# Self-attention scores of a unit on two disjoint row groups of TensorE

## The chip, the cores and the metric

One core of one Trainium2 chip runs the kernel in a single launch. The metric is the device time of that core in microseconds (us). TensorE multiplies a stationary operand (loaded first, "PEld" in the profile) with a moving one (the matmul, "PE") into PSUM; VectorE (DVE), ScalarE (ACT) and GpSimd (POOL) work beside it, and SyncE (SP) issues the DMAs. Each engine takes its instructions in the order in which the kernel lists them and waits on semaphores.

## What is computed

Two layers of cross-attention run over x (4 batches, 1024 tokens, 512 features). The first layer attends to a context of 64 tokens. The second has a self-attention, an attention to the context and a gated feed-forward part. The change is in the self-attention, which the reference writes as (16 heads of 32 features, batch `b`, queries `i`, keys `j`):

```python
q = (x @ wq).reshape(b, n, H, DH).transpose(0, 2, 1, 3)      # DH = 32
k = (ctx @ wk).reshape(b, m, H, DH).transpose(0, 2, 1, 3)    # here ctx is x's own norm h1
sim = jnp.einsum('bhid,bhjd->bhij', _fq(q, dq, 128.0, 8), _fq(k, dk, 128.0, 8)) * SCALE
attn = jax.nn.softmax(sim, axis=-1)
out = jnp.einsum('bhij,bhjd->bhid', _fq(attn, dw, 0.0, 8), _fq(v, dv, 128.0, 8))
```

`_fq` rounds to 8-bit integers. The kernel keeps these integers of queries and keys as bf16.

## The kernel before

**Chunks.** The tokens are cut into 8 chunks of 512 (`CHUNKS`), two per batch, numbered n = 0 to 7. For each batch the program runs `cross(n)` for both of its chunks (first layer, norm, and the products q1, k1, v1), then for each of the two `self_attention(n)` and `middle(n)` (output product, second attention, norm). The feed-forward part of chunk n-1 is spread over `self_attention(n)` and `middle(n)`, by a plan written out by hand (`HOST`, `feed`); so chunk 0 has none beside it, and chunks 1 to 7 are called hosted here.

**Layout.** q1 and k1 stand as [128 rows, 4 groups, 1024 tokens]: a row is one feature, four heads of 32 rows make a group. Row 32h of group hg is where head 4*hg+h begins. So a score product has 32 rows of stationary queries (128 queries wide) and 32 rows of moving keys (512 keys).

**Self-attention.** A unit is one head and 128 queries against 1024 keys; a chunk has 64 units and 71 slots (`S_SLOTS`). In slot s the engines do, in order:
- TensorE (line 1711 on): two score products of unit s (line 1725), one per 512 keys, into two adjacent PSUM banks (0 and 1, or 2 and 3, by turns); eight transposes of unit s-5 (line 1734) into the one bank 4; in two slots of four, 16 small products with the values (line 1748); then the feed-forward quarters of the plan, each three products of 512 columns (lines 1461 to 1463). The score products wait until the exponential of unit s-2 has emptied their banks.
- VectorE (line 1335 on): the row maximum of unit s (line 1341), every second slot the scale and reciprocal of the sums (1347, 1349), and the copy of the transposed unit s-5 out of bank 4 (1360).
- ScalarE (line 1051 on): negated maximum (1056), exponential (1062), and feed-forward work.
- GpSimd (line 785 on): the product with the reciprocal (791).

**Rounding of q1, k1, v1** (`cross`, line 1322 on): ScalarE scales a finished product of 128x512 out of PSUM into one of two buffers `qt` (line 929), and VectorE takes it in two passes (`take_rounded`, 1188 and 1190) into q1, k1 or v1.

**The SP queue.** SyncE issues all loads in program order: weight blocks into three slots of SBUF (`load_block`, lines 536 to 550), feed-forward pieces (559, 560), and, for the first chunks, a preparation of weights: `load_prep` (613) loads, ScalarE (978) and GpSimd (743) split into a high and a low part, and `keep_prep` (626) stores. `cross(1)` ends with `keep_prep` of the eighth weight, and `self_attention(0)` begins with the block "o1" and the load of the ninth.

**An older pairing in the same kernel.** In the setup, `three_of_heads` (line 1513, the product at 1518) alternates between rows 0 to 63 and rows 64 to 127, each into a bank of its own.

Of the kernel before, what the change touches and what calls it, by code (L numbers as in the profile page):

```python
# [7 lines left out]
BF16 = mybir.dt.bfloat16  # L8
FP16 = mybir.dt.float16
ALU = mybir.AluOpType  # L10
# [3 lines left out]
P = 128  # L14
# [3 lines left out]
DK0, DH = 64, 32  # L18
CH = 512
NC = S // CH  # L20
# [3 lines left out]
HG = H // 4  # L24
FF = 2048
FT = FF // P
KEYT = S // P
UNITS = HG * NT * 4
CHUNKS = B * NC
STEPS0 = 2 * NT  # L30

ROUND = 12582912.0
# [15 lines left out]
PIECES = 2 * len(F_ORDER)  # L48
F_RING = 3
PIECE_END = [4 * (v // 2) + (3 if F_ORDER[v // 2][0] == "d" else 2 * (v % 2) + 1) for v in range(PIECES)]  # L50


LAG_T = 5
# [145 lines left out]
def build(nc, a, out):  # L199

    ctx = ExitStack()
    with ctx:
        def sb(name, shape, dt=F32):
            return ctx.enter_context(nc.sbuf_tensor(name, shape, dt))
# [4 lines left out]
        def signal(name, keys, by=1):  # L209
            return Signal(sem(name), keys, by)  # L210
# [84 lines left out]
        for i in range(F_RING):  # L295
# [11 lines left out]
        qt = [qt0, qt1]  # L307
        NE, NH = 5, 3
        bufs = scope([(f"e1_{i}", [P, S], F32) for i in range(NE)] + [(f"w1b_{i}", [P, S], FP16) for i in range(NH)]
                     + [(f"w1T_{i}", [P, KEYT, P], BF16) for i in range(8)])  # L310
        e1, w1b, w1T = bufs[:NE], bufs[NE:NE + NH], bufs[NE + NH:]
        bufs = scope([(f"e2_{i}", [P, H, SC], F32) for i in range(NT)] + [("q2T", [P, HG, CH], BF16)]
                     + [(f"w2b_{i}", [P, H * SC], FP16) for i in range(2)] + [(f"w2T_{i}", [P, PAIRS, P], BF16) for i in range(2)])
        e2, q2T, w2b, w2T = bufs[0:NT], bufs[NT], bufs[NT + 1:NT + 3], bufs[NT + 3:]
        sb("upper", [P, 44 * 256])

        w_hi, w_lo = [w0_hi, w1_hi, w2_hi], [w0_lo, w1_lo, w2_lo]
        psum = ctx.enter_context(nc.psum_tensor("psum", [P, 8, 512], F32))
# [27 lines left out]
        f_loaded = [sem(f"f_loaded{i}") for i in range(F_RING)]  # L346
        fbias_loaded = [sem(f"fbias_loaded{i}") for i in range(3)]
        batch_loaded = signal("batch_loaded", range(B), 7 * 16)
        p0_used = signal("p0_used", [(n, i) for n in chunks for i in range(NT)])
        w1T_used = signal("w1T_used", [(n, g) for n in chunks for g in range(UNITS // 4) if g % 4 < 3])  # L350
        xhi_done = signal("xhi_done", [(n, k) for n in chunks for k in range(KT)])
# [38 lines left out]
        def bank_of(key):  # L390
            return FILL[key][0]

        def bank(i):
            return psum[:, i, :]
# [6 lines left out]
        def wait_emptied(eng, key):  # L401

            i, n = FILL[key]
            eng.wait_ge(emptied[i], n + 1)
# [55 lines left out]
        def _(sp):  # L460
# [167 lines left out]
            def cross(n):  # L628

                b, c = divmod(n, NC)  # L630
                if c == 0:
                    load_batch(b)
                    load_x(n)
                for i in range(3):
                    load_fbias(n, i)
                if n == 0:
                    load_block((0, "M0"))
                    load_block((0, "N0"))
                    load_block((0, "M1"))
                if c == 0:  # L640
                    load_x(n + 1)
                if n < NC:
                    load_prep(PREP[4 * n])
                for i in range(3, 7):
                    load_fbias(n, i)
                load_block((n, "N1"))
                if n < NC:
                    keep_prep(PREP[4 * n])
                    load_prep(PREP[4 * n + 1])
                load_fbias(n, 7)  # L650
                load_block((n, "q1"))
                load_block((n, "k1"))
                if n < NC:
                    keep_prep(PREP[4 * n + 1])
                    load_prep(PREP[4 * n + 2])
                load_block((n, "v1"))
                if n < NC:
                    keep_prep(PREP[4 * n + 2])
                    load_prep(PREP[4 * n + 3])
                if c == 0:  # L660
                    load_block((n + 1, "M0"))
                    load_block((n + 1, "N0"))
                    load_block((n + 1, "M1"))
                elif n > NC:
                    wait_filled(sp, ("q1", n, 3))
                    for v in range(F_RING):
                        load_piece(n - 2, v)
                if n < NC:
                    keep_prep(PREP[4 * n + 3])

            def self_attention(n):

# [10 lines left out]
            def middle(n):  # L683

                last_of_batch = n % NC == NC - 1
                if n == 0:
                    for v in range(F_RING):
                        load_piece(0, v)
                for s in range(M_SLOTS):
                    if n >= 1:  # L690
                        feed(n - 1, HOST, S_SLOTS + s, not last_of_batch or n == CHUNKS - 1)
                    if s == 4:
                        load_block((n, "o2"))
                    if s == 10 and last_of_batch and n + 1 < CHUNKS:
                        load_block((n + 1, "M0"))
                    if s == 18 and n + 1 < CHUNKS:
                        if last_of_batch:
                            load_block((n + 1, "N0"))
                if n >= 1:
                    store_out(n - 1)  # L700
                if last_of_batch and n + 1 < CHUNKS:
                    load_block((n + 1, "M1"))
# [412 lines left out]
        def _(dve):  # L1115
# [104 lines left out]
            def quantise(key, dst):  # L1220

                r = rounds[0]
                rounds[0] += 1
                take_rounded(key, qt[r % 2][:], dst).then_inc(rounded.sem, 1)

            def residual(key, xt):

                wait_filled(dve, key)
                return emptied_bank(dve.tensor_tensor(xt, bank(bank_of(key)), xt, ALU.add), key)  # L1229
# [44 lines left out]
            def cross(n):  # L1274
# [47 lines left out]
                for m in range(HG):  # L1322
                    quantise(("q1", n, m), q1[:, m, here])
                for m in range(HG):
                    quantise(("k1", n, m), k1[:, m, here])
                for t in range(NT):
                    quantise(("v1", n, t), v1[:, n % NC * NT + t, :])

# [112 lines left out]
        def _(pe):  # L1441
# [9 lines left out]
            def wait_bank(i, key):  # L1451

                n = sum(1 for k in FILL if FILL[k][0] == i and ORDER[k] < ORDER[key])
                pe.wait_ge(emptied[i], n)
# [256 lines left out]
            def self_attention(n):  # L1711

                last = n // NC * NC + NC - 1
                pe.wait_ge(rounded.sem, rounded.at(("v1", last, 3)))
                wait_bank(1, ("s1", n, 0))
                wait_bank(3, ("s1", n, 0))
                for s in range(S_SLOTS):
                    if s < UNITS:

                        hg, t, h = s // 16, s // 4 % 4, s % 4  # L1720
                        p = slice(DH * h, DH * h + DH)
                        q = n % NC * CH + t * P
                        wait_empty(("s1", n, s))
                        for i in range(2):
                            ins = pe.matmul(bank(bank_of(("s1", n, s)) + i), q1[p, hg, q:q + P], k1[p, hg, 512 * i:512 * i + 512],  # L1725
                                            start=True, stop=True)
                        done(ins, ("s1", n, s))
                    u = s - LAG_T
                    if 0 <= u < UNITS:
                        key = ("p1T", n, u)  # L1730
                        pe.wait_ge(w1_ready.sem, w1_ready.at((n, u)))
                        wait_empty(key)
                        for k in range(KEYT):
                            ins = pe.transpose(bank(bank_of(key)).bitcast(FP16)[:, k * P:k * P + P],  # L1734
                                               w1b[u % NH][:, k * P:k * P + P], ident16[:])
                        done(ins, key)
                    g, part = divmod(s - LAG_T - 4, 4)
                    if 0 <= g < UNITS // 4 and part < 2:
                        hg, t = divmod(g, 4)
                        key = ("a1", n, hg)  # L1740
                        if part == 0:
                            wait_emptied(pe, ("p1T", n, 4 * g + 3))
                            if t == 0:
                                wait_empty(key)
                        for k in range(4 * part, 4 * part + 4):
                            for h in range(4):
                                hd = DH * (4 * hg + h)
                                ins = pe.matmul(bank(5)[DH * h:DH * h + DH, t * P:t * P + P], v1[:, k, hd:hd + DH],  # L1748
                                                w1T[4 * (g % 2) + h][:, k, :], start=(k == 0), stop=(k == KEYT - 1))
                        if part == 1:  # L1750
                            if t == 3:
                                done(ins, key)
                            else:
                                ins.then_inc(w1T_used.sem, 1)
                    if n >= 1:
                        feed(n - 1, HOST, s)
# [108 lines left out]
```

## Time and profile before

| | |
|---|---|
| median of 3 runs | 3900.94 us (3900.22 to 3907.26) |
| the profiled execution, its own time | 3903.09 us |
| its span, first to last instruction | 3901.3 us |
| mean granted clock of TensorE | 0.872 of 2.4 GHz |

The profile counts as busy only compute instructions, and the end of a matmul is modelled, so that successive matmuls overlap in it. "Granted clock" 1.00 is 2.4 GHz and 0.50 is 1.2 GHz. "x2" merges two instructions of the same kind that follow each other. "<-" names what ended an engine's idle time. The chain of waits follows the work back from the last instruction.

### The profile page before, as it was taken

What the parts mean: (1) busy time and instruction counts of PE and PEld (TensorE: products, weight loads), DVE (VectorE), ACT (ScalarE), POOL (GpSimd) and SP (SyncE); (2) the same over time, 40 slices, a digit from 0 to 9 for tenths busy, and PEclk for the clock granted to TensorE, in tenths of its full rate; (3) what the DMA queues carried; (4) which work ended last, traced back from release to release, by engine and by line L of the source; (5) the groups of instructions that cost most, each with busy time, mean ns of one, the idle gap of its engine ahead of it and who ended that gap; (6) DMA issues with size and microseconds to landing.
All of it is one profiled execution on the core that took longest, in us unless ns stands there. A gap on an engine that the chain in (4) does not pass through costs nothing.

```text
span 3901.3 us, 50803 instructions
## 1 busy us (share of the span) xinstructions
PE 3174.2 (81%) x19712; PEld 2210.8 (57%) x19712; DVE 2174.1 (56%) x3559; ACT 1624.8 (42%) x2666; POOL 1328.8 (34%) x1025
## 2 busy tenths in 40 slices
PE   4445658789968799989967799889977799989989
PEld 4334433445656555655756655655756555655767
DVE  2324538667455567467445557467455567467431
ACT  3312136447422267357422257346422267357421
POOL 1231326344331234244241234244231244244231
PEclk8677765669988889999988879989988899999999
DMA  6873543312343322322344322322343322322334
GB/s 211 287 279 154 191 172 130 130 54 77 130 150 138 133 105 77 140 103 82 150 136 150 132 76 76 141 98 77 131 151 142 133 98 76 141 108 77 133 127 173
DMA packets 227694, 514.00 MB, mean 132 GB/s; under 512 B 96512, under 2 KB 113152, under 8 KB 205440
## 3 DMA queue, kind: packets, MB, share of 16 engines
q1 hardware_dynamic: 215040, 509.14, 35.8%
q10 hardware_dynamic: 12416, 1.62, 0.3%
q8 instruction: 158, 2.59, 0.3%
q14 instruction: 80, 0.66, 0.1%
HBM read 428.39 MB, written 82.31 MB: 131 GB/s over the span
## 4 chain that ended last, share of the span: by engine, by line
PE 62%; DVE 13%; issue 7%; POOL 6%; ACT 5%; DMA 4%; SPq 2%; ACTq 1%; POOLq 0%; DVEq 0%
PE psum L1461 17%; PE psum L1462 15%; PE psum L1463 15%; PE psum L1734 6%; PE psum L1725 6%; DVE mx L1341 2%; PE psum L1748 2%; DVE stats L1233 1%; POOL w1b L791 1%; DMA kept<-st_lo 1%; DVE w1T L1360 1%; POOL rstd L749 1%; DVE x L1229 1%; DVE den L1347 1%; ACT e L1062 1%
## 5 line engine op out<-in xcount | busy, mean ns | idle before, releaser
L791 POOL TENSOR_SCALAR w1b<-e,rec 128x1024 f16<-128x1024 f32 x512 | 572.8, 1119 | 903.9 <-DVE rec L1349 751.0
L1341 DVE TENSOR_REDUCE mx<-psum 128x1 f32<-128x1024 f32 x512 | 625.5, 1222 | 326.6 <-PE psum L1725 323.0
L1062 ACT ACTIVATE e<-psum,nb,scale 128x1024 f32<-128x1024 f32 x512 | 616.6, 1204 | 16.7
L1461 PE MATMUL psum<-h_hi,fw_hi 128*128 128x512 f32 x1024 | 463.7, 453 | 2.1 <-DVE h_lo L1152 2.1
L1734 PEld LDWEIGHTS psum<-ident,w1b 128*128 128x128 f16 x4096 | 264.6, 106 | 329.7 <-issue 261.7
L1725 PE MATMUL psum<-k,q 32*128 32x512 bf16 x1024 | 355.6, 432 | 103.3 <-ACT e L1062 83.2
L1463 PE MATMUL psum<-h_hi,fw_lo 128*128 128x512 f32 x1024 | 422.1, 412 | 0.0
L1462 PE MATMUL psum<-h_lo,fw_hi 128*128 128x512 f32 x1024 | 421.3, 411 | 0.0
L1734 PE MATMUL psum<-ident,w1b 128*128 128x128 f16 x4096 | 356.7, 237 | 72.1 <-DVE w1T L1360 60.7
L1360 DVE TENSOR_SCALAR w1T<-psum 128x1024 bf16<-128x1024 f16 x512 | 347.1, 678 | 44.2 <-PE psum L1734 42.8
L1461 PE MATMUL psum<-w_hi,ht_hi 128*128 128x512 f32 x640 | 268.8, 420 | 74.2 <-DVE e L1287 39.4
L1056 ACT ACTIVATE nb<-mx,nscale 128x1 f32<-128x1 f32 x512 | 150.0, 293 | 410.1 <-DVE mx L1341 409.2
L1229 DVE TENSOR_TENSOR x<-psum,x 128x512 f32<-128x512 f32 x224 | 152.6, 684 | 272.2 <-PE psum L1463 272.2
L1462 PE MATMUL psum<-w_lo,ht_hi 128*128 128x512 f32 x640 | 260.7, 407 | 0.0
L1463 PE MATMUL psum<-w_hi,ht_lo 128*128 128x512 f32 x640 | 259.1, 405 | 0.0
L1461 PE MATMUL psum<-fw_hi,u_hi 128*128 128x512 f32 x512 | 229.9, 449 | 21.4 <-POOL u_lo L800 15.9
L749 POOL TENSOR_TENSOR rstd<-ve,mhalf 128x1 f32<-128x1 f32 x128 | 87.0, 679 | 467.7 <-DVE ve L1237 467.7
L1461 PEld LDWEIGHTS psum<-h_hi,fw_hi 128*128 128x128 f32 x1024 | 203.1, 198 | 74.3 <-issue 27.0
L1152 DVE TENSOR_TENSOR ht_lo<-psum,ht_hi 128x512 fp32r<-128x512 f32 x160 | 108.2, 689 | 222.5 <-ACT psum L985 121.8
L1463 PEld LDWEIGHTS psum<-h_hi,fw_lo 128*128 128x128 f32 x1024 | 204.3, 200 | 48.1
L1725 PEld LDWEIGHTS psum<-k,q 32*128 32x128 bf16 x1024 | 57.5, 95 | 297.1 <-issue 183.9
L1462 PEld LDWEIGHTS psum<-h_lo,fw_hi 128*128 128x128 f32 x1024 | 205.7, 201 | 27.9
(165 smaller groups left out, 5763.5 us busy)
## 6 DMA issues: line engine op xcount, KB each, us to landing
fw_hi<-pieces SPq DMA_DIRECT2D x192, 512.0 KB, 3.2
fw_lo<-pieces SPq DMA_DIRECT2D x192, 512.0 KB, 4.2
w_hi<-kept SPq DMA_DIRECT2D x80, 1024.0 KB, 4.9
w_lo<-kept SPq DMA_DIRECT2D x80, 1024.0 KB, 7.4
fbias<-in_fside_Bx16xSxS SPq DMA_DIRECT2D x64, 256.0 KB, 4.1
prep_raw<-in_L_xattn_ff_w SPq DMA_DIRECT2D x12, 1024.0 KB, 8.1
pieces<-prep_hi SPq DMA_DIRECT2D x24, 512.0 KB, 3.6
pieces<-prep_lo SPq DMA_DIRECT2D x24, 512.0 KB, 5.6
```

The lines of the kernel that those rows point to most:

```text
L749: pool.tensor_tensor(rstd[:, t:t + 1], ve[:, t:t + 1], mhalf[:, t:t + 1], ALU.pow).then_inc(rstd_ready.sem, 1)
L791: pool.tensor_scalar(w1b[u % NH][:], e1[u % NE][:], rec1[:, u % 8:u % 8 + 1], HALF, ALU.mult, ALU.add).then_inc(w1_ready.sem, 1)
L1056: act.activation(nb1[:, s % 4:s % 4 + 1], mx1[:, s % 4:s % 4 + 1], ACT.Copy, scale=nscale[:, 0:1]).then_inc(nb_ready.sem, 1)
L1062: act.activation(e1[s % NE][:], psum[:, i:i + 2, :].rearrange("p i n -> p (i n)"), ACT.Exp, bias=nb1[:, s % 4:s % 4 + 1], scale=scale[:, 0:1],
L1229: return emptied_bank(dve.tensor_tensor(xt, bank(bank_of(key)), xt, ALU.add), key)
L1341: dve.tensor_reduce(mx1[:, s % 4:s % 4 + 1], psum[:, i:i + 2, :].rearrange("p i n -> p (i n)"), AX, ALU.max).then_inc(maxed1.sem, 1)
L1360: emptied_bank(dve.tensor_scalar(w1T[u % 8][:].rearrange("p k q -> p (k q)"), bank(bank_of(key)).bitcast(FP16), -HALF, W_HIGH, ALU.add, AL ...
L1461: pe.matmul(o, s_hi, m_hi, start=first, stop=False)
L1462: pe.matmul(o, s_hi, m_lo, start=False, stop=False)
L1463: return pe.matmul(o, s_lo, m_hi, start=False, stop=last)
L1725: ins = pe.matmul(bank(bank_of(("s1", n, s)) + i), q1[p, hg, q:q + P], k1[p, hg, 512 * i:512 * i + 512], start=True, stop=True)
L1734: ins = pe.transpose(bank(bank_of(key)).bitcast(FP16)[:, k * P:k * P + P], w1b[u % NH][:, k * P:k * P + P], ident16[:])
```

## The change

The second half of the keys (k1, columns 512 to 1023, the odd chunk of a batch) is stored 64 rows further on, modulo 128. A new buffer `q1_turned` holds a copy of the chunk's queries with their rows turned by 64 too. It shares SBUF with the end of weight slot 1. The two products of a unit then read rows 32h and 32(h^2): for h = 0 rows 0 to 31 and 64 to 95. The copy is made by two DMAs of SyncE per chunk (`turn_queries`); TensorE waits for them at the start of `self_attention`. The turned keys are rounded by three VectorE passes in place of two (`quantise_turned`).

```diff
--- before.py
+++ after.py
@@ -307,12 +310,12 @@
         qt = [qt0, qt1]
         NE, NH = 5, 3
         bufs = scope([(f"e1_{i}", [P, S], F32) for i in range(NE)] + [(f"w1b_{i}", [P, S], FP16) for i in range(NH)]
-                     + [(f"w1T_{i}", [P, KEYT, P], BF16) for i in range(8)])
-        e1, w1b, w1T = bufs[:NE], bufs[NE:NE + NH], bufs[NE + NH:]
+                     + [(f"w1T_{i}", [P, KEYT, P], BF16) for i in range(8)] + [("q1_turned", [P, HG, CH], BF16)])
+        e1, w1b, w1T, q1_turned = bufs[:NE], bufs[NE:NE + NH], bufs[NE + NH:-1], bufs[-1]
         bufs = scope([(f"e2_{i}", [P, H, SC], F32) for i in range(NT)] + [("q2T", [P, HG, CH], BF16)]
                      + [(f"w2b_{i}", [P, H * SC], FP16) for i in range(2)] + [(f"w2T_{i}", [P, PAIRS, P], BF16) for i in range(2)])
         e2, q2T, w2b, w2T = bufs[0:NT], bufs[NT], bufs[NT + 1:NT + 3], bufs[NT + 3:]
-        sb("upper", [P, 44 * 256])
+        sb("upper", [P, 46 * 256])
 
         w_hi, w_lo = [w0_hi, w1_hi, w2_hi], [w0_lo, w1_lo, w2_lo]
         psum = ctx.enter_context(nc.psum_tensor("psum", [P, 8, 512], F32))
@@ -346,6 +349,7 @@
         f_loaded = [sem(f"f_loaded{i}") for i in range(F_RING)]
         fbias_loaded = [sem(f"fbias_loaded{i}") for i in range(3)]
         batch_loaded = signal("batch_loaded", range(B), 7 * 16)
+        q1_turned_loaded = signal("q1_turned_loaded", range(CHUNKS), 32)
         p0_used = signal("p0_used", [(n, i) for n in chunks for i in range(NT)])
         w1T_used = signal("w1T_used", [(n, g) for n in chunks for g in range(UNITS // 4) if g % 4 < 3])
         xhi_done = signal("xhi_done", [(n, k) for n in chunks for k in range(KT)])
@@ -667,6 +671,17 @@
                         load_piece(n - 2, v)
                 if n < NC:
                     keep_prep(PREP[4 * n + 3])
+                if c == NC - 1:
+                    wait_block_used(sp, (n, "k1"))
+                    sp.wait_ge(rounded.sem, rounded.at(("q1", n, 3)))
+                    turn_queries(n - 1)
+
+            def turn_queries(n):
+
+                cs = slice(n % NC * CH, n % NC * CH + CH)
+                for h in range(2):
+                    sp.dma_start(q1_turned[64 * h:64 * h + 64, :, :], q1[64 - 64 * h:128 - 64 * h, :, cs]
+                                 ).then_inc(q1_turned_loaded.sem, 16)
 
             def self_attention(n):
 
@@ -691,6 +706,9 @@
                         feed(n - 1, HOST, S_SLOTS + s, not last_of_batch or n == CHUNKS - 1)
                     if s == 4:
                         load_block((n, "o2"))
+                    if s == 12 and not last_of_batch:
+                        wait_block_used(sp, (n, "q2"))
+                        turn_queries(n + 1)
                     if s == 10 and last_of_batch and n + 1 < CHUNKS:
                         load_block((n + 1, "M0"))
                     if s == 18 and n + 1 < CHUNKS:
@@ -1222,6 +1240,18 @@
                 r = rounds[0]
                 rounds[0] += 1
                 take_rounded(key, qt[r % 2][:], dst).then_inc(rounded.sem, 1)
+
+            def quantise_turned(key, dst):
+
+                r = rounds[0]
+                rounds[0] += 1
+                buf = qt[r % 2]
+                wait_emptied(dve, key)
+                link(dve.tensor_scalar(buf[:], buf[:], -ROUND, Q_HIGH, ALU.add, ALU.min))
+                landed()
+                link(dve.tensor_scalar(dst[0:64], buf[64:128, :], Q_LOW, None, ALU.max))
+                landed()
+                dve.tensor_scalar(dst[64:128], buf[0:64, :], Q_LOW, None, ALU.max).then_inc(rounded.sem, 1)
 
             def residual(key, xt):
 
@@ -1322,7 +1352,10 @@
                 for m in range(HG):
                     quantise(("q1", n, m), q1[:, m, here])
                 for m in range(HG):
-                    quantise(("k1", n, m), k1[:, m, here])
+                    if n % NC == 0:
+                        quantise(("k1", n, m), k1[:, m, here])
+                    else:
+                        quantise_turned(("k1", n, m), k1[:, m, here])
                 for t in range(NT):
                     quantise(("v1", n, t), v1[:, n % NC * NT + t, :])
 
@@ -1712,18 +1745,21 @@
 
                 last = n // NC * NC + NC - 1
                 pe.wait_ge(rounded.sem, rounded.at(("v1", last, 3)))
+                pe.wait_ge(q1_turned_loaded.sem, q1_turned_loaded.at(n))
                 wait_bank(1, ("s1", n, 0))
                 wait_bank(3, ("s1", n, 0))
                 for s in range(S_SLOTS):
                     if s < UNITS:
 
                         hg, t, h = s // 16, s // 4 % 4, s % 4
-                        p = slice(DH * h, DH * h + DH)
                         q = n % NC * CH + t * P
                         wait_empty(("s1", n, s))
-                        for i in range(2):
-                            ins = pe.matmul(bank(bank_of(("s1", n, s)) + i), q1[p, hg, q:q + P], k1[p, hg, 512 * i:512 * i + 512],
-                                            start=True, stop=True)
+                        i = bank_of(("s1", n, s))
+                        p = slice(DH * h, DH * h + DH)
+                        turned = slice(DH * (h ^ 2), DH * (h ^ 2) + DH)
+                        pe.matmul(bank(i), q1[p, hg, q:q + P], k1[p, hg, 0:512], start=True, stop=True)
+                        ins = pe.matmul(bank(i + 1), q1_turned[turned, hg, t * P:t * P + P], k1[turned, hg, 512:1024],
+                                        start=True, stop=True)
                         done(ins, ("s1", n, s))
                     u = s - LAG_T
                     if 0 <= u < UNITS:
```

## Rows read from the trace of the kernel before

**Rows 1.** The page: span, busy time of the engines, its share, instructions.
```profile
span 3901.3 us, 50803 instructions
PE 3174.2 (81%) x19712; PEld 2210.8 (57%) x19712; DVE 2174.1 (56%) x3559; ACT 1624.8 (42%) x2666; POOL 1328.8 (34%) x1025
```

**Rows 2.** Chain of waits, by line: the whole span, then windows 526:723 and 1387:1565.
```profile
by line: PE psum L1461 16.9%; PE psum L1462 14.8%; PE psum L1463 14.8%; issue 6.8%; PE psum L1734 5.9%; PE psum L1725 5.8%; DVE mx L1341 2.1%; PE psum L1748 2.0%; DVE stats L1233 1.4%; POOL w1b L791 1.3%; DMA kept<-st_lo 1.1%; DVE w1T L1360
...
by line: PE psum L1725 15.0%; DVE mx L1341 13.7%; issue 12.1%; PE psum L1734 11.6%; DVE den L1347 10.8%; DMA prep_raw<-in_L_xattn_ff_w 9.3%; DVE w1T L1360 4.9%; POOL prep_lo L743 4.6%; PE psum L1748 4.2%; ACT prep_hi L978 4.1%; SPq L626 2.9
...
by line: PE psum L1725 16.1%; PE psum L1461 15.8%; PE psum L1734 14.4%; PE psum L1463 11.8%; PE psum L1462 11.7%; issue 7.9%; PE psum L1748 4.8%; POOL w1b L791 4.6%; DVE mx L1341 4.1%; ACT gate L1020 2.1%; DVE w1T L1360 1.7%; ACT e L1062 1.
```

**Rows 3.** Busy time in stretches: the score loops of chunks 0, 2 and 3.
```profile
core 0: us, PE busy (x) PEld busy (x) DVE busy (x) ACT busy (x) POOL busy (x), PEclk, DMA share, GB/s
526.00:723.00 197.00, 133.72 (x1042) 62.49 (x1043) 141.78 (x186) 116.69 (x203) 112.80 (x71) 0.50 0.42 150
...
1387.00:1565.00 178.00, 166.05 (x1340) 95.36 (x1338) 131.80 (x199) 126.52 (x223) 82.39 (x70) 0.92 0.23 83
1699.00:1873.00 174.00, 161.32 (x1341) 93.21 (x1342) 133.09 (x202) 128.53 (x227) 82.53 (x70) 0.95 0.27 98
```

**Rows 4.** Timeline at clock 1.00 and 0.50; last, durations of line 1725 (min/median/max).
```profile
1502.10 0.60 PE L1725 MATMUL psum<-k,q 32*128 32x512 bf16 x2
...
1502.63 0.45 PEld L1734 LDWEIGHTS psum<-ident,w1b 128*128 128x128 f16 x8 [0.42 <-issue]
...
643.02 1.03 PE L1725 MATMUL psum<-k,q 32*128 32x512 bf16 x2
...
L1725 PE MATMUL psum<-k,q x1024: 374/384/629, 526.0 to 3626.4; 32*128 32x512 bf16 x171
```

**Rows 5.** Timeline of the setup's pairs (line 1518), and plain products at clock 0.50.
```profile
122.49 0.66 PE L1518 MATMUL psum<-ps_lo,v_hi 64*128 64x512 f32 x2
122.92 0.66 PE L1518 MATMUL psum<-ps_hi,v_lo 64*128 64x512 f32 x2
...
1164.46 0.63 PE L1462 MATMUL psum<-w_lo,ht_hi 128*128 128x512 f32 x1
1164.89 0.63 PE L1463 MATMUL psum<-w_hi,ht_lo 128*128 128x512 f32 x1
...
L1518 PE MATMUL psum<-ps_lo,v_hi x32: 392/625/628, 122.5 to 171.2; 64*128 64x512 f32 x32
```

**Rows 6.** Waits in 1387:1565: waiting engine, releaser, us in total, times, longest.
```profile
DVE mx L1341 <- PE psum L1725: 38.4, 42, 3.1
```

**Rows 7.** Groups of instructions in the whole trace: busy, mean ns; idle before.
```profile
L1341 DVE TENSOR_REDUCE mx<-psum 128x1 f32<-128x1024 f32 x512 | 625.5, 1222 | 326.6 <-PE psum L1725 323.0
...
L1360 DVE TENSOR_SCALAR w1T<-psum 128x1024 bf16<-128x1024 f16 x512 | 347.1, 678 | 44.2 <-PE psum L1734 42.8
```

**Rows 8.** Timeline: VectorE rounds one product of k1 in cross(3).
```profile
1366.84 0.43 DVE L1188 TENSOR_SCALAR k<-qt 128x512 bf16<-128x512 f32 x1 [1.97 <-ACT qt L929]
1367.30 0.29 DVE L1190 TENSOR_SCALAR k<-k 128x512 bf16<-128x512 bf16 x1
```

**Rows 9.** Chain of waits in 542:568: start, us, what; last, a DMA issue of the page.
```profile
544.17 4.51 POOL prep_lo L743
...
552.06 1.16 SPq L549
...
554.91 10.57 DMA prep_raw<-in_L_xattn_ff_w
...
565.50 1.91 ACT prep_hi L978
...
fbias<-in_fside_Bx16xSxS SPq DMA_DIRECT2D x64, 256.0 KB, 4.1
```

**Rows 10.** Line 1725 in stretches of hosted loops at half and at full clock.
```profile
815.00:848.00 33.00, 9.24 (x18) 1.13 (x18) 0.50 0.11 41
939.00:1005.00 66.00, 14.85 (x50) 2.71 (x50) 1.00 0.27 97
```

## The prediction

> **What bounds the kernel now.** I read the page first, then the chain of waits, then the score loops by stretch, then single units. TensorE is busy for 3174 of 3901.3 us, against 2174 for VectorE and 1625 for ScalarE [rows 1]. Such shares average over stages, so the chain decides: the score products of line 1725 hold 5.8% of it, 0.058 x 3901.3 = 226 us [rows 2]. In the loop of chunk 0 they hold 15.0% of 197 us = 29.6 us, which leaves 196 us for the seven hosted loops; chunk 2 alone has 16.1% of 178 = 28.7 us [rows 2]. In that hosted loop TensorE is busy 166 of 178 us, VectorE 132, ScalarE 127; in chunk 0 TensorE is at 134 of 197, at a granted clock of 0.50, against 0.92 and 0.95 in chunks 2 and 3 [rows 3]. So the hosted loops are bound by TensorE, with VectorE some 34 us behind it, and chunk 0 by a round trip through all engines.
>
> **One pair now.** At clock 1.00 the two products of a unit take 0.60 us together, and the weight load of the next transposes begins 0.53 us after the pair's start [rows 4]. One product alone lasts 0.37 us at the least (that includes its way through the array) [rows 4], so the second starts 0.60 - 0.37 = 0.23 us after the first. At clock 0.50 it is 1.03 - 0.63 = 0.40 us [rows 4]. What the change can remove is this distance.
>
> **Part 1: disjoint rows.** The trace has no 32-row pair in different rows, but the setup's pairs of 64-row products are near: two products of 512 columns take 0.66 us where one lasts 0.625, so the second starts 0.03 us later, and the next pair follows 0.43 us after the first [rows 5]. At the same clock of 0.50 two plain products of that size stand 0.43 us apart [rows 5]: a pair costs what one product costs. The bounds for the new distance are therefore 0.03 us (the second runs beside the first) and 0.23/0.40 us (it doesn't). I take 0.03, since those rows have the same number of columns and also write two banks. Saved per pair: 0.20 us at full clock, 0.37 at half. The transposes, which use all rows, still wait for both.
>
> How much lies on the path? Hosted: 196 us of chain, of which the share 0.20/0.53 goes = 74 us. Chunk 0: a cold pair holds about 1.03 - 0.06 = 0.97 us of chain, so 29.6 x 0.37/0.97 = 11 us. Sum 85 us. Not all of it is kept, for VectorE is next. Of the 64 row maxima in chunk 2, 42 waited for the scores, 38.4 us in all [rows 6]; there the earlier score is worth its full time. The other 22 found VectorE late, and I give them half: (42 + 11)/64 = 0.83. So 85 x 0.83 = **70 us**.
>
> The floor beneath it: VectorE's loop needs 64 x (1.222 + 0.678) = 122 us for maxima and copies [rows 7], and is busy 132 in all [rows 3]. With its waits outside the scores (178 - 132 - 38 = 8 us) that is 140 us. The forecast leaves about 178 - 9 = 169, so the floor isn't reached, but in slots with one feed-forward quarter VectorE already sets the pace.
>
> The Trainium skill ("TensorE: Matmul & The Clock Gate", Part 3, "The mechanism" and "Measured speedup vs the span model") has tiles on different rows start about 4 ns apart, less than the 0.03 us of [rows 5]. With its figure the hosted chain would give 196 x 0.226/0.53 = 84 us and chunk 0 12 us, 80 us kept in all. The second section has 3.07x for four tiles of 32 rows, not 4x; were two tiles to fall short as much (77%), a full-clock pair would save only 0.46 - 0.46/1.54 = 0.16 us, an estimate that makes it about 56 us. I stay with the rows.
>
> **Part 2: three rounding passes.** On one product of k1 VectorE now spends 0.43 + 0.29 us after 1.97 us of idleness [rows 8], once per 2.7 us. The new passes have no row of their own: each lies between 0.29 us (the pass bf16 to bf16) and twice the 0.43 us pass, as each works on f32 and two on half the rows. That makes 0.9 to 2.6 us against the 2.69 us of a period: nothing as long as the products pace it, and at worst a fraction of a microsecond at the last k1 product of four chunks. I take 0; at the upper bound 16 x 1.9 = 30 us of VectorE time would still stand in its own idleness, some 2 us of it visible.
>
> **Part 3: the turned queries.** Eight times, SyncE issues two DMAs of 64 rows x 4 KB, 256 KB each, like the bias loads that land after 4.1 us [rows 9]; 4 MB beside 514 MB moved. For the second chunk of a batch they go out in slot 12 of `middle(n)`, behind q2's products: ten slots of other work cover them. SyncE's feed loads behind them wait for later TensorE steps anyway. For the first chunk of batches 1 to 3 they go out when the k1 products are done, with four v1 products (4 x 2.7 us) still to run; "o1", next in the queue, waits for v1 longer than that. Cost 0. If the cover went, TensorE would stand some 4 us per chunk.
>
> Chunk 0 is different, and it is the queue that matters. There `keep_prep` of the eighth weight stands ahead of the copy, and it waits for GpSimd's split, which begins at 544.17 us and takes 4.51 [rows 9]. So the copy goes out at 552.06, where the "o1" loads go out now, and the first scores, at 526.0 today [rows 4], come at about 557: 30 us later. But ScalarE didn't get to the first exponential before 544 either, and after four units it waited for the ninth weight, whose load was issued at 554.91 and let the split begin at 565.50 [rows 9]. Late scores at 557 plus four units at some 2.6 us give 567.5. The other way, two more issues ahead of the load, 0.3 to 1.2 us each (the row of "o1" shows 1.16), give 566 to 568. Both agree: **+2 us**, bounds 0 and +12 (the copy takes as long as the 10.57 us load).
>
> **Sum.** 3903.1 (the profiled execution's own time, 2 us above its span and above the median) - 70 + 2 = 3835 us. Against the median of 3901 that is 3833; I say 3834.
>
> **The rivals.**
> *A. VectorE becomes the bound sooner.* A third of the maxima already find VectorE late, and the PSUM pair gives it only two units of slack. If only half of the 74 + 11 us were kept: 3901 - 43 + 2 = 3860 us; with a third, 3875. For it: VectorE's 132 us; against it: its 38 us of waiting on scores. Chance 0.24.
> *B. The products don't run beside each other*, because 32-row tiles differ from the 64-row ones or since the row is read from matmul ends that are modelled. Then only part 3 is left: 3901 + 2 = 3903. Against it, the pairs follow each other at 0.43 us, which isn't an end but a start. Chance 0.05.
> *C. Slower: the clock.* Place: the hosted loops. At half clock 9 units took 33 us, 3.7 us each; at full clock 25 took 66, 2.6 each [rows 10]. A unit at half clock costs 1.1 us more. Clock 0.50 held through chunk 0, where TensorE had the least work in a loop [rows 3]. The change takes work off TensorE. If the hosted loops lose more than 70/1.1 = 64 units (of 448) to half clock, all is given back; their mean clock would fall by about 0.5 x 64 x 3.7/(7 x 178) = 0.10. With twice that, 128 units, the time is 3901 - 68 + 141 = 3974. Against it: the loops shorten with the work, so the busy share should stay near 0.9. The Trainium skill (the same page, Part 1, "What's actually happening") says that throttled is the default and activity releases it; by that rule less work on TensorE speaks for C. Chance 0.09, two thirds of it beyond the break-even.
> The opposite may also come: half-clock stretches that end sooner, 10 to 20 us more of gain.
>
> **How the numbers follow.** The forecast (concurrent, most of it kept) has 0.62, A 0.24, B 0.05, C 0.09. The forecast's own range is 3800 (the full 85 us, and 17 us of clock) to 3855. The range for all reaches to A's lesser end: 3798 to 3875; outside are B, most of C and a little on the low side. A measurement of this kernel tells 0.2%, 8 us, from no change. Faster: 0.62 + 0.24 + 0.03 of C = 0.89; same: B, 0.05; slower: 0.06.
>
> **What would show it.** The pair of line 1725 should read about 0.40 to 0.42 us at full clock and 0.66 at half, in place of 0.60 and 1.03, and the transposes' weight load should begin 0.33 us after the pair. Busy time of line 1725 should come to about 512 x 0.42 = 215 us. Hosted loops should take 162 to 172 us where chunk 2 took 178, with VectorE's waits on scores down from 38 us to about 28 and TensorE's waits on VectorE's copies up. In chunk 0 the first score should stand near 557 and the ninth split near 567. Wrong would be: second products still 0.2 us or more behind the first (B), hosted loops of the old length with a VectorE that no longer waits (A), or a mean clock well below 0.92 in them (C).

## The result and the profile after

The changed kernel takes 3793.7 us (3791.9 to 3794.8, 4 runs) against 3900.6: a ratio of 0.973, interval 0.971 to 0.976. That is 107 us less, where 67 less was forecast, and 4 us below the low end of the range.

The page of the changed kernel: span and busy times, then the groups of the score products (line 1725 is now 1760 and 1761) and of the row maximum (busy us, mean ns; idle before it).

```profile
span 3791.2 us, 50839 instructions
PE 3003.7 (79%) x19712; PEld 2180.3 (58%) x19712; DVE 2182.8 (58%) x3575; ACT 1621.5 (43%) x2666; POOL 1328.7 (35%) x1025
...
L1374 DVE TENSOR_REDUCE mx<-psum 128x1 f32<-128x1024 f32 x512 | 624.6, 1221 | 216.9 <-PE psum L1761 214.4
...
L1760 PE MATMUL psum<-k,q 32*128 32x512 bf16 x512 | 214.8, 421 | 116.0 <-ACT e L1080 63.1
```

TensorE's busy time fell by 171 us, the maxima's waits for scores from 323 to 214 [rows 7]. One unit in the timeline, at full clock:

```profile
1477.44 0.38 PE L1760 MATMUL psum<-k,q 32*128 32x512 bf16 x1
1477.45 0.38 PE L1761 MATMUL psum<-k,q_turned 32*128 32x512 bf16 x1
1477.77 0.62 PE L1770 MATMUL psum<-ident,w1b 128*128 128x128 f16 x8
```

The second product starts within 0.01 us of the first, and the transposes 0.33 us after the pair, where it was 0.53 [rows 4]. Over the whole trace the commonest value is 0.32, so a pair that nothing else holds up is worth 0.21 us at full clock.

The loops, from first to last score, in stretches: of the kernel before, chunks 0, 1, 2 and 4 (the time, then TensorE's busy time and its granted clock).

```profile
526.00:722.00 196.00, 132.72 (x1039) 0.50 0.42 151
816.30:1004.60 188.30, 175.22 (x1339) 0.87 0.19 68
1386.70:1563.90 177.20, 165.75 (x1338) 0.92 0.23 84
...
2254.00:2441.50 187.50, 174.47 (x1338) 0.87 0.21 79
```

And of the changed kernel, the same chunks:

```profile
557.50:716.00 158.50, 105.44 (x1038) 0.52 0.43 152
809.00:973.20 164.20, 145.31 (x1338) 0.96 0.22 78
1355.50:1519.10 163.60, 144.92 (x1338) 0.97 0.24 90
...
2204.00:2366.10 162.10, 144.27 (x1340) 0.98 0.25 91
```

Here is the surprise. Chunks 1 and 4 gained 24 and 25 us, chunk 2 14, chunk 3 only 5: those gained most that had spent the longest at half clock, and their clock rose from 0.87 to 0.96 and 0.98. I call 2 x (1 - clock) x length the half-clock time of a loop. Summed over the seven hosted loops it fell from 218 to 103 us, and the loops together from 1253.8 to 1154.6 us, 99 less. (The profile gives the clock to two decimals, which makes such a sum good to about 3 us.) Chunk 0 ended 6 us sooner; of the 110 us between the two spans, some 5 fell in the stages between.

What did the pair itself bring? Units 36 to 64 of chunk 2 (28 steps) run wholly at full clock in every kernel of this study but the last, for which chunk 3 is taken. Before, and changed:

```profile
1489.53:1563.94 74.41, 69.90 (x638) 1.00 0.24 86
```
```profile
1448.25:1519.13 70.88, 64.21 (x638) 1.00 0.25 90
```

3.53 us in 28 steps is 0.126 per unit, 60% of the 0.21; the same stretch reads 74.4 and 70.9 us in all seven hosted loops. Scaled to 63 steps and seven loops it makes 56 us, so 43 of the 99 have another source. Step by step, over the 60 steps of a loop that run at full clock somewhere in both traces, the gain is 7.1 us a loop, or 50 in all; that leaves 49. Units at half clock save more by the pair than the others: 218/3.7 = 59 units at 0.37 in place of 0.21 would be another 9 us, an estimate from [rows 10] and the prediction's own 0.37. So the rest is 43 to 49 us, and 34 at the very least. The clock was the suspect; it could have been an accident of alignment, a consequence of shorter loops, or of more rows at work.

### The profile page after: what moved, and what is told of

It is laid out like the page before. It is cut to its first block, busy times and chain, and to the rows that moved or that the text cites. A ratio compares the mean times of both kernels' runs of the same rounds, so it can differ in the third digit from the quotient of the medians.

```text
span 3791.2 us, 50839 instructions
## 1 busy us (share of the span) xinstructions
PE 3003.7 (79%) x19712; PEld 2180.3 (58%) x19712; DVE 2182.8 (58%) x3575; ACT 1621.5 (43%) x2666; POOL 1328.7 (35%) x1025
## 4 chain that ended last, share of the span: by engine, by line
PE 58%; DVE 18%; issue 7%; ACT 6%; POOL 6%; DMA 4%; SPq 2%; ACTq 1%; POOLq 0%; DVEq 0%
PE psum L1494 16%; PE psum L1495 15%; PE psum L1496 15%; PE psum L1770 5%; DVE mx L1374 4%; PE psum L1760 3%; DVE w1T L1393 2%; PE psum L1784 2%; DVE stats L1263 1%; DVE den L1380 1%; DMA kept<-st_lo 1%; ACT e L1080 1%; DVE x L1259 1%; POOL rstd L767 1%; SPq L502 1%
## 5 line engine op out<-in xcount | busy, mean ns | idle before, releaser
L1494 PE MATMUL psum<-h_hi,fw_hi 128*128 128x512 f32 x1024 | 452.7, 442 | 2.2 <-DVE h_lo L1170 2.2
L1770 PE MATMUL psum<-ident,w1b 128*128 128x128 f16 x4096 | 348.1, 234 | 126.2 <-DVE w1T L1393 115.1
L1495 PE MATMUL psum<-h_lo,fw_hi 128*128 128x512 f32 x1024 | 411.2, 402 | 0.0
L1496 PE MATMUL psum<-h_hi,fw_lo 128*128 128x512 f32 x1024 | 411.0, 401 | 0.0
L1760 PE MATMUL psum<-k,q 32*128 32x512 bf16 x512 | 214.8, 421 | 116.0 <-ACT e L1080 63.1
L1760 PEld LDWEIGHTS psum<-k,q 32*128 32x128 bf16 x512 | 47.0, 92 | 300.2 <-issue 198.3
L818 POOL TENSOR_TENSOR u_lo<-gate,u_hi 128x512 fp32r<-128x512 f32 x128 | 164.3, 1284 | 154.1 <-ACT u_hi L1024 148.4
```

The source lines that it names most:

```text
L818: pool.tensor_tensor(u_lo[:, m, :], gate[:, m, :], u_hi[:, m, :].bitcast(F32), ALU.subtract).then_inc(u_lo_done.sem, 1)
L1494: pe.matmul(o, s_hi, m_hi, start=first, stop=False)
L1495: pe.matmul(o, s_hi, m_lo, start=False, stop=False)
L1496: return pe.matmul(o, s_lo, m_hi, start=False, stop=last)
L1760: pe.matmul(bank(i), q1[p, hg, q:q + P], k1[p, hg, 0:512], start=True, stop=True)
```

## The experiments

The table has the median, the hosted loops' total, their half-clock time (both from the stretches of each profile, as above) and the stretch of 28 steps. The kernels ran in five series. The kernel before ran in each, with medians of 3893 to 3907 us, and the ratios in the text are against those.

| kernel | median us | hosted loops | half clock | 28 steps |
|---|---|---|---|---|
| before | 3900.6 | 1253.8 | 218 | 74.4 |
| changed | 3793.7 | 1154.6 | 103 | 70.9 |
| rows only (+64) | 3794.6 | 1157.8 | 109 | |
| rows only (+32) | 3793.3 | 1154.5 | 116 | |
| changed, same rows | 3920.3 | 1273.8 | 260 | |
| half the columns | 3792.3 | 1156.2 | 109 | 70.9 |
| 64 rows, in turn | 3843.2 | 1202.6 | 93 | 74.5 |
| 128 rows, in turn | 3811.2 | 1171.1 | 77 | 72.2 |
| 64 + 64 rows at once | 3788.2 | 1150.6 | 92 | |
| before, half maximum | 3854.8 | 1205.7 | 162 | 71.9 |
| changed, half maximum | 3734.5 | 1096.8 | 104 | 67.2 |
| changed, reciprocal on GpSimd | 3776.1 | 1134.1 | 110 | 69.4 (chunk 3) |

**Rows without copies.** In the kernel before:

```diff
-                            ins = pe.matmul(..., q1[p, hg, q:q + P], k1[p, hg, 512 * i:512 * i + 512],
+                            r = slice(DH * (h ^ 2 * i), DH * (h ^ 2 * i) + DH)
+                            ins = pe.matmul(..., q1[r, hg, q:q + P], k1[r, hg, 512 * i:512 * i + 512],
```

> The kernel before, but the second score product of a unit takes queries and keys of the head 64 rows further on, straight from q1 and k1: no turned copy, no third rounding pass, no DMA. The second 512 scores of each unit are those of another head. If parts 2 and 3 of the change cost nothing but the 2 us of chunk 0, the time is 3791 us (3793.7 less 2), the pair reads 0.39 to 0.40 us and the mean granted clock is 0.884. If the copies and passes hide a cost or a wait, it is below 3785.

Measured: 3794.6 us (3788.1 to 3795.8), ratio 0.973 (0.971 to 0.975), the same as the change. In chunk 0 the last score stands at 713.4 us, with the copies at 716.0: the 2 to 3 us of part 3. They don't show in the median. With `h ^ i` in place of `h ^ 2 * i`, the rows 32 further on:

> As the run with rows only, but the second product uses the rows 32 further on (32(h^1)) in place of 64. If any two disjoint groups of 32 rows work beside each other, it gives the same as that run, 3792 to 3796 us, and the second product starts 0.01 to 0.03 us after the first. If only groups in different halves do, the pair reads 0.60 us again and the time is 3900.

3793.3 us, ratio 0.973 (0.970 to 0.976), and the second product again starts 0.003 us after the first: groups of 32 rows next to each other do as well as groups 64 rows apart. Groups 96 rows apart were not run.

**The change without its rows.**

```diff
-                        pe.matmul(bank(i), q1[p, hg, q:q + P], k1[p, hg, 0:512], start=True, stop=True)
+                        pe.matmul(bank(i), q1_turned[turned, hg, t * P:t * P + P], k1[turned, hg, 0:512], start=True, stop=True)
```

> The changed kernel, but the first score product takes the same rows as the second (q1_turned and k1 at the turned rows). The first 512 scores are those of another head. Copies, passes and waits all stay. If the row groups carry the whole gain, the time is that of the kernel before plus 2 us, 3903, the pair reads 0.60 and 1.03 us, and the mean clock falls back to 0.872 with some 218 us of half clock in the hosted loops. If something else in the change (the other order of waits, the shifted start of chunk 0) brought part of the gain, it is 3880 or less.

3920.3 us (ten runs, 3879.3 to 3926.4), ratio 1.004 (1.001 to 1.007). So the rows carry the whole gain. It is 17 us slower than expected; in its profile the half-clock time is 260 us, not 218. The stretches of its chunks 1 and 2:

```profile
822.00:1010.10 188.10, 175.19 (x1339) 0.87 0.19 68
1392.40:1579.90 187.50, 174.43 (x1338) 0.87 0.21 79
```

Chunk 2 takes 187.5 us at 0.87 here and 177.2 at 0.92 before, with the same work: where products are serial on 32 rows, a loop comes in longer and shorter forms. The single runs bear it out. The ten of this kernel reach from 3879 us at a mean clock of 0.876 to 3926 at 0.865. Those of the kernel before reach from 3884 at 0.877 to 3916 at 0.867 (the lowest of all, 3876, is without a clock). The changed kernel's ten runs lie within 3792 and 3798 at 0.882 to 0.885. With 2 x (1 - clock) x time as the half-clock time of a run, these two pairs of ends differ by 0.48 and 0.37 us for each us more at half clock.

**Half the columns**, on the same rows, one after the other:

```diff
-                            ins = pe.matmul(bank(bank_of(("s1", n, s)) + i), ..., k1[p, hg, 512 * i:512 * i + 512],
+                            ins = pe.matmul(bank(bank_of(("s1", n, s)) + i)[:, 0:256], ..., k1[p, hg, 512 * i:512 * i + 256],
```

> The kernel before with both score products of a unit on the same rows, but 256 columns wide in place of 512 (half of the keys' scores are left out). The pair takes TensorE about as long as the concurrent pair does. Theory 'time': full clock comes back sooner because the pair takes less of the slot and the full-array feed-forward products more; then this gives the same as the change, 3785 to 3800 us, mean clock 0.884. Theory 'rows': it matters that two row groups work at once; then the clock stays near 0.872, and only the gain at full clock is left, about 50 us in the hosted loops and 8 in chunk 0, 3840 us. Theory 'chance': the clock of single runs scatters and the mean over the runs lies between.

3792.3 us, ratio 0.973 (0.971 to 0.975), half-clock time 109. "Rows" as stated falls: no second group at work is needed. A pair that is shorter brings both the 28 steps (70.9) and the clock. "Chance" falls too: none of these loops has the long form, and the four runs lie within 4 us at a mean clock of 0.883 to 0.885.

**More rows, nothing shorter.** First all rows (`q1[:, hg, ...]`, `k1[:, hg, ...]`), then 64 (`r = slice(64 * (h // 2), 64 * (h // 2) + 64)`), in both cases the two products one after the other.

> The kernel before, but both score products use all 128 rows of the group (so the scores are sums over four heads); same count, same columns, same order, nothing beside each other. The pair should still read 0.60 us. Theory 'rows': more rows at work keep or bring back the full clock, hosted half-clock time falls from 218 us towards 100 and the time to about 3865. Theory 'time': nothing changes in TensorE's time, 3901 us and a mean clock of 0.872. A small gain of 0.1 us per change between 32-row and 128-row products, if there is one, would show as a shorter way from the pair to the transposes (0.53 us now).

> The kernel before, with each score product on 64 rows in place of 32 (sums over two heads), both on the same rows, so one after the other. It tells apart why the run with all 128 rows gained 86 us. If that came from doing without the change between products on part of the rows and on all (0.10 us before the pair and 0.04 behind it), the gaps stay here and the time stays near 3900, mean clock 0.872. If the number of rows at work brings back the full clock, half-clock time in the hosted loops falls from 215 us to 80 to 150, the loops at full clock stay as long as before, and the time is 3830 to 3870.

All rows: 3811.2 us, ratio 0.978 (0.976 to 0.980). That mixes two things, for the 28 steps fell by 2.2 us too. Its timeline shows why: the pair starts 0.24 us after the last feed-forward product, and the transposes 0.44 us after the pair, the commonest values of its hosted loops.

```profile
1467.52 0.40 PE L1463 MATMUL psum<-h_hi,fw_lo 128*128 128x512 f32 x1
1467.76 0.60 PE L1725 MATMUL psum<-k,q 128*128 128x512 bf16 x2
1468.20 0.61 PE L1734 MATMUL psum<-ident,w1b 128*128 128x128 f16 x8
```

With 64 rows the gaps are those of before, 0.32 to 0.33 and 0.53 us:

```profile
1463.54 0.39 PE L1463 MATMUL psum<-fw_hi,u_lo 128*128 128x512 f32 x1
1463.86 0.60 PE L1726 MATMUL psum<-k,q 64*128 64x512 bf16 x2
1464.39 0.62 PE L1735 MATMUL psum<-ident,w1b 128*128 128x128 f16 x8
```

So is the stretch of 28 steps, 74.5 us. Yet the time is 3843.2, ratio 0.986 (0.983 to 0.989), and chunks 1 and 2 read

```profile
814.00:985.80 171.80, 159.51 (x1338) 0.97 0.20 74
1367.20:1538.30 171.10, 158.76 (x1338) 0.97 0.23 87
```

This isolates the clock: the same instructions, lengths and gaps, only more rows in use, and the hosted loops take 51 us less with 125 us less at half clock, 0.41 us for each. "Time" as the only cause falls here. In the change, 115 us less at half clock are then worth 0.41 x 115 = 47 us, beside the 43 to 49 left over above.

**Both at once**: 64 rows in one half of the array beside 64 in the other (`64 * (h // 2 ^ i)`).

> The kernel before, with the two products of a unit on 64 rows each, the first in one half of the array and the second in the other (sums over two heads), no copies. The pair should read 0.39 us at full clock, as with 32 rows each, so the slots at full clock are those of the run with rows only (149.5 us for 60 slots). Only the rows at work differ, 128 in place of 64. If their number still helps the clock, half-clock time in the hosted loops falls below the 109 us of that run, to 60 to 90, and the time to 3775 to 3785; if what is left at half clock comes from other stalls (the Gelu waits), it stays near 100 and the time at 3790.

3788.2 us, ratio 0.973 (0.970 to 0.975), half clock 92 us, where 64 rows in turn had 93. More rows beside each other bring the hosted loops little.

Chunk 0, which has no feed-forward products, tells more of the rows. Its stretch with half the columns, with 64 rows in turn and with all rows in turn:

```profile
524.50:711.70 187.20, 106.09 (x1039) 0.51 0.44 158
530.20:720.70 190.50, 122.05 (x1039) 0.58 0.44 155
526.30:709.40 183.10, 97.68 (x1039) 0.76 0.45 161
```

Its clock was 0.50 before and 0.52 in the changed kernel. So a shorter pair, by columns or by two products at once, did next to nothing for the clock here, while more rows raised it to 0.58, 0.59 (64 + 64 at once) and 0.76. Each is one profile. The two levers of the hosted loops are not of equal worth everywhere.

**What held back the other slots.** The maximum over the first 512 scores only, in both kernels:

```diff
-                        dve.tensor_reduce(mx1[:, s % 4:s % 4 + 1], psum[:, i:i + 2, :].rearrange("p i n -> p (i n)"),
+                        dve.tensor_reduce(mx1[:, s % 4:s % 4 + 1], psum[:, i, 0:512],
```

> The kernel before, with VectorE's row maximum taken over the first 512 of a unit's 1024 scores only (about 0.6 us less per unit; the second half of the maximum is left out). If the hosted loops before are bound by TensorE in nearly all slots, they shorten little at full clock, under 5 us each, and chunk 0 shortens most. Time about 3860.

> The changed kernel with the same halved maximum. If VectorE is what held back the other slots (in the changed kernel about 4 in 10 slots gained nothing at full clock where the rest gained 0.21 us), then with VectorE relieved the change is worth its full distance: the hosted loops at full clock are 63 x 0.21 = 13 us each shorter than those of the kernel before with the halved maximum, against 7 us without it. Time 3860 less 13 x 7 and less the clock's share, 3725 to 3750. If something else held them back, the difference stays at 7 us a loop.

3854.8 us (ratio 0.988, 0.985 to 0.992) and 3734.5 (0.958, 0.955 to 0.961). The change is now worth 120 us in place of 107, and 4.8 us in the 28 steps (71.9 to 67.2) in place of 3.5. Over the 59 steps that run at full clock in both profiles in some loop, 51 gained 0.18 us or more, 11.7 us a loop; with the whole maximum it is 30 of 60, and 7.1 us. So VectorE held back most of the others. The sums close: the pair's 11.7/59 x 63 x 7 = 87 us and 0.41 x 58 = 24 for the clock (162 to 104 us at half clock) make 111 where the hosted loops lost 109. With the whole maximum 7.1/60 x 63 x 7 = 52 and 47 make 99, where they lost 99.

**Two tries to do better.** The first: the copy of chunk 0 ahead of the stores of the eighth weight (the `if c == NC - 1` block moved up). It ran beside the changed kernel itself.

> The changed kernel itself, for comparison on the same chip with the two below: 3792 to 3795 us.

> The changed kernel, but SyncE issues the first chunk's turned copy ahead of the eighth weight's stores in place of behind them. In chunk 0 the first scores should then stand near 541 us in place of 557.5. If the ninth weight's load is what chunk 0 waits for there, only the two issues leave that path: the split of the ninth weight starts 2 to 3 us sooner and the time falls by 2 to 3 us. If the late scores themselves cost the time, it falls by up to 14 us.

3794.3 us against 3794.7: nothing. The chain of waits in chunk 0, of this run:

```profile
534.49 11.41 DMA prep_raw<-in_L_xattn_ff_w
...
558.21 10.36 DMA prep_raw<-in_L_xattn_ff_w
...
568.60 1.91 ACT prep_hi L996
```

and of the changed kernel:

```profile
533.53 7.89 DMA prep_raw<-in_L_xattn_ff_w
...
555.83 10.80 DMA prep_raw<-in_L_xattn_ff_w
...
566.66 1.91 ACT prep_hi L996
```

The first scores came at 546.9 us in place of 557.5, but the copy now flies beside the eighth weight's load, which takes 11.4 us where the two profiles of the changed kernel have 7.9 and 7.7. That uses up the two issues saved: the split of the ninth weight begins at 568.60, against 566.66 and, in the second profile of the changed kernel, 568.62. The second: VectorE's scale and reciprocal moved to GpSimd.

```diff
-                        link(dve.tensor_scalar(den1[:, at], sum1[:, at], delta[:, 3:4], None, ALU.mult))
-                        landed()
-                        dve.reciprocal(rec1[:, at], den1[:, at]).then_inc(rec_ready.sem, 1)
+                    pool.tensor_scalar(den1[:, at], sum1[:, at], delta[:, 3:4], None, ALU.mult).then_inc(den_ready.sem, 1)
+                    pool.wait_ge(den_ready.sem, den_ready.at((n, u // 2)))
+                    pool.tensor_tensor(rec1[:, at], den1[:, at], minus1[:], ALU.pow).then_inc(rec_ready.sem, 1)
```

> The changed kernel with the two small VectorE instructions of every second unit (scale of the sums and reciprocal, 0.35 and 0.17 us, and the wait between them) moved to GpSimd (product and power of -1). If VectorE holds back the slots that gained nothing, each hosted loop at full clock shortens by 3 to 6 us and the time falls by 20 to 45 us. If GpSimd's power instruction (0.68 us where it is used for the norms) comes on the path instead, the time stays or rises.

3776.1 us (3774.9 to 3777.5), ratio 0.968 (0.965 to 0.971): faster than both kernels. The power instruction takes 710 ns, but GpSimd is at 112 of 160 us:

```profile
1354.00:1514.00 160.00, 144.55 (x1338) 91.50 (x1338) 119.82 (x136) 124.84 (x222) 112.03 (x130) 0.96 0.25 91
```

## Why the prediction was wrong

**The step that failed** is the clock: the sum has no term for it. Rival C read "less work on TensorE" as a danger to the full clock; its last sentence has the direction that came, but at "10 to 20 us more", of which 17 us went into the low end and none into the forecast. It was 43 to 49 us in the gain's direction by the counts above, and 34 at the least. Chunk 1 stood at 0.87, and at 0.50 in its first 33 us. [rows 10] shows line 1725 alone there; all of TensorE was busy for 31.7 of them:

```profile
815.00:848.00 33.00, 31.66 (x91) 0.50 0.11 41
```

So its idleness wasn't what kept the clock down; I used these 33 us only for a price. The runs show what did: much of the time went to products that use 32 rows of the array. Use more rows (64 in turn) or spend less time in them (half the columns) and the half-clock time of the hosted loops halves either way.

**Part 1** was right in kind: the pair costs what one product costs. Of its size, the distance is 0.003 us (median of the trace's 512 pairs), not 0.03, and the chain gave 74 us x 0.83 = 61 for the hosted loops; priced at full clock 50 to 56 came. Chunk 0 was to end 11 x 0.83 - 2 = 7 us sooner and did so by 6. The Trainium skill's 4 ns ("TensorE: Matmul & The Clock Gate", Part 3, "The mechanism") was nearer than my row of 64-row pairs. The Trainium skill's 3.07x for four tiles (the same page, "Measured speedup vs the span model") isn't tested here, as no run has four. The shortfall that I scaled from it to two tiles didn't come: the pair takes 0.38 us where one product takes 0.37 at the least.

**Rival A** was partly right. VectorE kept back 40% of the distance at full clock, more than my 17% of the chain's share; but I had counted only the pairs on the chain, so the two came to about the same. In chunk 2 its waits on scores fell from 38 to 24 us (28 forecast), and TensorE's waits on its copies rose from 4 to 10.

**Part 2**: three passes of 0.43, 0.42 and 0.42 us, within the bounds, and hidden; idle time before the first is 1.38 us in place of 1.97 [rows 8].

```profile
1343.77 0.43 DVE L1250 TENSOR_SCALAR qt<-qt 128x512 f32<-128x512 f32 x1 [1.38 <-ACT qt L947]
1344.23 0.42 DVE L1252 TENSOR_SCALAR k<-qt 64x512 bf16<-64x512 f32 x1
1344.69 0.42 DVE L1254 TENSOR_SCALAR k<-qt 64x512 bf16<-64x512 f32 x1
```

**Part 3** was right in its times: the first scores stood at 557.5 us (557 forecast), the split of the ninth weight began at 566.66 (567), the copy landed after 4.4 us in the median. Its +2 us can't be told from nothing: without the copies chunk 0 ended 2.6 us sooner, and the median was no lower.

**Rival B** is out: the start times show it, and the time too.

Left open: which mix of rows and time grants the full clock. The runs show two levers, not a rule.

## What to carry to other kernels

Where two products use few rows, put them on disjoint rows. The second was free here where nothing but TensorE held the slot, with groups 32 and 64 rows apart. Then ask what the granted clock does, loop by loop, before pricing a change to TensorE's work: chunk 1 took 188.3 us at 0.87 and, with 64-row products of the same length, 171.8 at 0.97. And look for the engine that is next; moving two small instructions (0.27 us per unit) off VectorE was worth another 19 us (3794.7 to 3776.1).

## What was unexpected of the hardware

The clock followed the rows in use, not only TensorE's busy share: 218 us of half clock with 32-row products, 93 with 64-row products of the same length. In chunk 0 it was 0.50 with 32 rows, 0.58 with 64 and 0.76 with 128. A change between products on 32 or 64 rows and products on all costs about 0.09 us ahead of the pair (0.33 against 0.24) and 0.09 behind it (0.53 against 0.44), at full clock; the expectation of the 64-row run has 0.04 for the latter, from one slot that wasn't typical. And two copies of 256 KB issued just behind a load of 1 MB went with a load of 11.4 us in place of 7.7 to 7.9, in one profile.
